# A two-layer graph attention kernel: softmax probabilities and the first layer's output split in halves before a transpose by DMA, fp16 weight halves in layer two, and a new instruction order

## What is computed

```
q, k, v = x@Wq+bq, x@Wk+bk, x@Wv+bv                     # 6 heads of 64
p0  = softmax(q k^T / 8 + where(adj, 0, -9e15))
x1  = layernorm(x + (p0 v)@Wf + bf)
h   = x1 @ W1 ;  th = tanh(h)                           # 12 heads of 32
z   = leaky(src(th) + dst(th)^T, 0.2), -999 off the mask
f   = elu(softmax(z) h + b)
g   = sigmoid(x1 @ Hw^T + Hb)
out = layernorm(x1 + g*f + (1-g)*x1)
```

## Time and profile before

| what | value |
|---|---|
| runs | 1122.74, 1123.22, 1124.8 us; median 1123.22 |
| span of the profiled execution | 1121.2 us (no run time is listed for this execution) |
| PE busy | 1047.1 us, 93% |
| PEld busy | 950.8 us, 85% |
| DVE busy | 1025.2 us, 91% |
| POOL busy | 947.2 us, 84% |
| ACT busy | 893.5 us, 80% |
| DMA, share of 16 engines | 32.7% |
| one turn in the steady part | 32.65 us |

### The profile page before, as it was taken

One profiled execution on the slowest core, in us unless ns is written; L12 is line 12 of the kernel. 1 busy time (PEld: TensorE's weight loads), 2 busy tenths in 40 slices (PEclk: granted clock), 3 DMA queues, 4 the chain that ended last, 5 costly groups with the idle time before them and its releaser, 6 DMA issues.

```text
span 1121.2 us, 32794 instructions
## 1 busy us (share of the span) xinstructions
PE 1047.1 (93%) x10890; PEld 950.8 (85%) x10890; DVE 1025.2 (91%) x2138; ACT 893.5 (80%) x1739; POOL 947.2 (84%) x781
## 2 busy tenths in 40 slices
PE   4899999999999999999999999999999999999761
PEld 4888889889898988889898888889888888988641
DVE  5589999999999999999999999999999999999854
ACT  4568888888888888888888888888888888888753
POOL 2158889988888998888899888889988888998775
PEclk9899999999999999999999999999999999999975
DMA  6103333232333333234333323433332243332232
GB/s 200 32 21 73 98 84 89 76 86 66 82 97 83 89 79 84 70 79 97 83 89 81 82 74 74 97 83 89 83 82 77 69 97 83 93 81 72 47 67 73
DMA packets 188717, 91.33 MB, mean 81 GB/s; under 512 B 158864, under 2 KB 183696, under 8 KB 188688
## 3 DMA queue, kind: packets, MB, share of 16 engines
q1 hardware_dynamic: 188688, 90.95, 32.7%
HBM read 31.61 MB, written 12.58 MB: 39 GB/s over the span
## 4 chain that ended last, share of the span: by engine, by line
PE 73%; issue 9%; DVE 8%; POOL 4%; ACT 3%; DMA 1%; DVEq 0%; SPq 0%; POOLq 0%; ACTq 0%
PE lin L459 42%; PE zp L554 6%; PE zp L613 3%; PE zp L617 3%; PE fp L583 3%; PE tp L498 3%; PE tp L567 3%; PE tp L626 2%; DVE sd L1008 2%; PE tp L595 2%; PE fp L586 2%; PE fp L640 2%; ACT th L736 1%; ACT sd_t L765 1%; POOL z L1353 1%
## 5 line engine op out<-in xcount | busy, mean ns | idle before, releaser
L1353 POOL TENSOR_TENSOR z<-z,z_max 128x1536 f32<-128x1536 f32 x64 | 176.4, 2757 | 21.3 <-DVE z_max L1136 18.9
L818 ACT ACTIVATE z<-z,log_scale 128x1536 f32<-128x1536 f32 x64 | 101.3, 1583 | 53.7 <-POOL z L1353 53.6
L1360 POOL TENSOR_TENSOR p_lo<-z,p_hi 128x1024 f16<-128x1024 f32 x64 | 137.3, 2145 | 2.3 <-ACT p_hi L824 2.3
L1365 POOL TENSOR_TENSOR f<-f,x_kept 128x384 f32<-128x384 f32 x64 | 65.0, 1016 | 72.0 <-DVE f L1168 72.0
L1318 POOL TENSOR_TENSOR prod<-th,w_sd_rows 128x768 f32<-128x768 f32 x64 | 117.9, 1842 | 6.6 <-ACT th L736 6.4
L784 ACT ACTIVATE p<-p,p_min 128x128 f32<-128x128 f32 x384 | 118.9, 399 | 4.7 <-DVE p_min L1068 4.7
L1129 DVE SCALAR_TENSOR_TENSOR z<-zp,z 128x1536 f32<-128x1536 f32 x64 | 111.9, 1748 | 2.3 <-ACT z L793 2.3
L1136 DVE TENSOR_REDUCE z_max<-z 128x12 f32<-128x1536 f32 x64 | 111.6, 1744 | 0.1
L793 ACT ACTIVATE z<-zp 128x1536 f32<-128x1536 f32 x64 | 93.2, 1457 | 17.8 <-PE zp L617 17.8
L1331 POOL TENSOR_TENSOR v_part<-v_res,v_part 128x384 bf16<-128x384 f32 x64 | 63.0, 984 | 35.8 <-ACT v_part L755 33.8
L459 PE MATMUL lin<-xt_hi,Wq_hi 128*128 128x256 f32 x288 | 81.0, 281 | 12.7 <-DVE Wk_lo L926 12.4
(11 more groups left out here) (162 smaller groups left out, 4394.2 us busy)
## 6 DMA issues: line engine op xcount, KB each, us to landing
xt_raw<-x_t SPq DMA_DIRECT2D x32, 384.0 KB, 4.0
x_raw<-x SPq DMA_DIRECT2D x32, 384.0 KB, 3.2
x_kept<-x SPq DMA_DIRECT2D x64, 192.0 KB, 2.3
out<-out_tile SPq DMA_DIRECT2D x64, 192.0 KB, 1.9
adj<-adj SPq DMA_DIRECT2D x64, 32.0 KB, 1.9
dst_row<-sd_t SPq DMA_DIRECT2D x64, 9.0 KB
p1t_hi<-p_hi SPq DMA_TRANSPOSE x64, 3.2
p1t_lo<-p_lo SPq DMA_TRANSPOSE x64, 3.1
```

Source lines behind the costliest of these rows:

```text
L818: act.activation(z[:, g, :], z[:, g, :], ACT.Exp, bias=log_scale[:, :]).then_inc(z_exp[g].sem, 1)
L1353: pool.tensor_tensor(zs, zs, z_max[:, g, :].unsqueeze(2).to_broadcast([128, H1, N]), ALU.subtract)\
L1360: pool.tensor_tensor(p1_lo[:, g, :], z[:, g, PE_HEADS * N:], p1_hi[:, g, :], ALU.subtract).then_inc(w1_lo[g].sem, 1)
```

## The change

- Layer 0's probabilities are split before they are transposed: ACT makes the f16 high half from SBUF (768 columns), DVE the low half from SBUF (768 columns, `weights0_low`), and one DMA a graph transposes both halves (`turn_weights0`, 12 blocks). The PE transposes and the copies from PSUM go.
- x1 is scaled by 1024 and split in fp16, high half on ACT (`first_high`), low half on POOL (`first_low`), and one DMA a graph transposes both (`turn_x1`, 6 blocks). W1 and Hw become fp16 halves with a scale found from their maxima.
- Layer 1 splits all 12 heads before the transpose: ACT and POOL work on 1536 columns instead of 1024, the two DMAs a graph on 12 blocks instead of 8. The PE transposes of four heads and their copies go.
- The maximum is applied in two ways: POOL adds the negative maximum for 4 heads (512 columns), and for 8 heads ACT takes one exponential each with a bias per head. DVE makes that offset (`z_offsets`, 12 columns).
- The two layer norms are applied on DVE (`norm0`, `norm1`: one tensor_scalar with mean and deviation as pointers) instead of ACT; the shifts go. Epsilon and the power -1/2 are done for both graphs in one instruction each.
- The biases of gate and projection enter as one bf16 matmul of 384 columns ahead of the product; the rows are split in three bf16 parts at the start (`row_parts`, seven instructions each for `bf` and `Hb`, after one that prepares the row; `Hb` also one small one).
- The second adjacency load and its mask go; SP copies the mask and x1 from SBUF to SBUF instead (`keep_mask`, `copy_mask`, `hold_x1`, `keep_x1`).
- Five PSUM banks serve all products and transposes (`GEN_USERS`, `BANKS`) in place of three separate sets, and every engine's list is written anew; `turn.later` is two turns back.

The core of the diff (the lists of steps are left out; three places of them follow as orders):

```diff
-PE_HEADS, DMA_HEADS = 4, 8
+SUB_HEADS = 4
...
+GEN_USERS = ("ctx0", "qk2", "ct0", "qk1", "ctx1", "pr0", "ct1", "qk0", "pr1", "sdt", "f0", "v0", "v1", "f1", "g1", "h0", "g0", "h1")
+BANKS = {"h1": 1, "g0": 4, "qk0": 3, "f1": 2, "ctx0": 3, "ct0": 2, "ctx1": 2, "ct1": 2, "pr1": 2, "qk1": 3, "v1": 3, "h0": 2}
...
+                def turn_weights0(g):
+                    sp.wait_ge(p0_low[g].sem, now(p0_low[g]))
+                    turn.apart()
+                    sp.wait_ge(ctx_mm[g].sem, prev(ctx_mm[g]))
+                    turn.apart()
+                    sp.dma_start_transpose(p0t[:, g, :, :].rearrange("p i (a n) -> p (i a) n", a=H0),
+                                           p0_part[:, g, :, :].rearrange("p i n -> p (i n)"))\
+                        .then_inc(p0_turned[g].sem, 16)
...
+                def turn_x1(g):
...
+                    sp.dma_start_transpose(x1t[:, g, :, :, :].rearrange("p i c n -> p (i c) n"),
+                                           x1_part[:, g, :, :].rearrange("p i n -> p (i n)"))\
...
-                    sp.dma_start_transpose(p1t_hi[:, g, PE_HEADS * N:].rearrange("p (a n) -> p a n", a=DMA_HEADS),
+                    sp.dma_start_transpose(p1t_hi[:, g, :].rearrange("p (a n) -> p a n", a=H1),
...
+                def hold_x1(g):
+                    sp.wait_ge(x1_ready[g].sem, prev(x1_ready[g]))
+                    turn.apart()
+                    sp.wait_ge(x1_copied[g].sem, prev(x1_copied[g]))
+                    turn.apart()
+                    sp.dma_start(x1_held[:, g, :], x1[:, g, :]).then_inc(x1_moved[g].sem, 16)
...
+            def rows_product(out, hi, lo, name, bias=None):
+                if bias:
+                    pe.matmul(out[:, 0:D], ones_bf[:, :], bias_parts[bias][:, :], start=True, stop=False)
+                return product(out[:, 0:D], hi, lo, lambda k: w_hi[name][:, k, :], lambda k: w_lo[name][:, k, :], not bias)
...
+                def weights0_high(g):
+                    act.wait_ge(sc_exp[g].sem, now(sc_exp[g]))
+                    act.wait_ge(p0_turned[g].sem, prev(p0_turned[g]))
+                    act.activation(p0_part[:, g, 0, :], p0[:, g, :], ACT.Copy, scale=PSCALE).then_inc(p0_high[g].sem, 1)
...
-                def norm0(g):
...
-                    act.activation(x1[:, g, :], y[:, g, :], ACT.Identity, bias=shift0[:, g, :], scale=rstd[:, g, :])\
-                        .then_inc(x1_ready[g].sem, 1)
...
                 def z_exponent(g):
+                    act.wait_ge(z_offset[g].sem, now(z_offset[g]))
+                    for h in range(SUB_HEADS, H1):
+                        last = act.activation(z[:, g, N * h:N * (h + 1)], z[:, g, N * h:N * (h + 1)], ACT.Exp,
+                                              bias=z_off[:, g, h:h + 1])
+                    last.then_inc(z_exp1[g].sem, 1)
+
+                def z_exponent_rest(g):
                     act.wait_ge(z_sub[g].sem, now(z_sub[g]))
-                    act.activation(z[:, g, :], z[:, g, :], ACT.Exp, bias=log_scale[:, :]).then_inc(z_exp[g].sem, 1)
+                    act.activation(z[:, g, 0:SUB_HEADS * N], z[:, g, 0:SUB_HEADS * N], ACT.Exp).then_inc(z_exp[g].sem, 1)
 
...
-                    act.activation(p1_hi[:, g, :], z[:, g, PE_HEADS * N:], ACT.Copy).then_inc(w1_hi[g].sem, 1)
-
...
-                def weights0_low(g, half):
...
-                    dve.scalar_tensor_tensor(out=p0t_lo[:, g, c], in0=bank[:, 0:3 * N], scalar=PSCALE,
-                                             in1=p0t_hi[:, g, c], op0=ALU.mult, op1=ALU.subtract)\
...
+                def weights0_low(g):
+                    dve.wait_ge(p0_high[g].sem, now(p0_high[g]))
+                    dve.wait_ge(p0_turned[g].sem, prev(p0_turned[g]))
+                    dve.scalar_tensor_tensor(out=p0_part[:, g, 1, :], in0=p0[:, g, :], scalar=PSCALE,
+                                             in1=p0_part[:, g, 0, :], op0=ALU.mult, op1=ALU.subtract)\
+                        .then_inc(p0_low[g].sem, 1)
...
-                def shift_norm0(g):
...
-                    dve.tensor_scalar(shift0[:, g, :], moments[:, g, 0:1], rstd[:, g, :], -1.0, ALU.mult, ALU.mult)\
-                        .then_inc(norm0_shift[g].sem, 1)
...
+                def variance0():
+                    for g in range(2):
+                        dve.wait_ge(y_mom[g].sem, now(y_mom[g]))
+                    for g in range(2):
+                        dve.wait_ge(x1_ready[g].sem, prev(x1_ready[g]))
+                    dve.tensor_scalar(rstd[:, :, :], moments[:, :, 1:2], EPS, X1_SCALE ** -2, ALU.add, ALU.mult)\
+                        .then_inc(y_var.sem, 2)
+
+                def norm0(g):
+                    dve.wait_ge(y_rstd.sem, now(y_rstd))
+
+                    dve.wait_ge(x1_low[g].sem, now(x1_low[g]))
+                    dve.wait_ge(x1_moved[g].sem, now(x1_moved[g]))
+                    dve.tensor_scalar(x1[:, g, :], y[:, g, :], moments[:, g, 0:1], rstd[:, g, :], ALU.subtract, ALU.mult)\
+                        .then_inc(x1_ready[g].sem, 1)
...
+                def z_offsets(g):
...
+                    dve.tensor_scalar(z_off[:, g, :], z_max[:, g, :], -1.0, math.log(PSCALE), ALU.mult, ALU.add)\
+                        .then_inc(z_offset[g].sem, 1)
...
+                def norm1(g):
+                    dve.wait_ge(y2_rstd.sem, now(y2_rstd))
+
+                    dve.wait_ge(stored[g].sem, prev(stored[g]))
+                    dve.tensor_scalar(out_tile[:, g, :], y2[:, g, :], moments2[:, g, 0:1], rstd2[:, g, :], ALU.subtract,
+                                      ALU.mult).then_inc(out_ready[g].sem, 1)
...
+                def row_parts(name, done):
+                    row = bias_row[name]
+                    parts = bias_parts[name][:, :]
...
+                    dve.tensor_copy(first, row).then_inc(rows_split.sem, 1)
+                    dve.wait_ge(rows_split.sem, done + 1)
+                    dve.tensor_tensor(rest, row, first, ALU.subtract).then_inc(rows_split.sem, 1)
...
+                    dve.scalar_tensor_tensor(out=parts, in0=second, scalar=ident[:, 1:2], in1=parts, op0=ALU.mult,
+                                             op1=ALU.add).then_inc(rows_split.sem, 1)
+                    dve.wait_ge(rows_split.sem, done + 6)
+                    return dve.scalar_tensor_tensor(out=parts, in0=rest, scalar=ident[:, 2:3], in1=parts, op0=ALU.mult,
+                                                    op1=ALU.add)
...
+                    dve.tensor_tensor(bias_row["bf"], zp[:, 2, 0:D], bias_row["bf"], ALU.add).then_inc(rows_split.sem, 1)
+                    dve.wait_ge(rows_split.sem, 1)
+                    dve.wait_ge(consts_ready.sem, 3)
+                    row_parts("bf", 1).then_inc(bf_ready.sem, 1)
...
+                def first_low(g):
+                    pool.wait_ge(x1_high[g].sem, now(x1_high[g]))
+                    pool.wait_ge(x1_turned[g].sem, prev(x1_turned[g]))
+                    pool.tensor_tensor(x1_part[:, g, 1, :], x1[:, g, :], x1_part[:, g, 0, :], ALU.subtract)\
+                        .then_inc(x1_low[g].sem, 1)
...
-                    zs = z[:, g, :].rearrange("p (a n) -> p a n", a=H1)
-                    pool.tensor_tensor(zs, zs, z_max[:, g, :].unsqueeze(2).to_broadcast([128, H1, N]), ALU.subtract)\
+                    pool.wait_ge(z_offset[g].sem, now(z_offset[g]))
+                    zs = z[:, g, 0:SUB_HEADS * N].rearrange("p (a n) -> p a n", a=SUB_HEADS)
+                    pool.tensor_tensor(zs, zs, z_off[:, g, 0:SUB_HEADS].unsqueeze(2).to_broadcast([128, SUB_HEADS, N]), ALU.add)\
...
-                    pool.tensor_tensor(p1_lo[:, g, :], z[:, g, PE_HEADS * N:], p1_hi[:, g, :], ALU.subtract).then_inc(w1_lo[g].sem, 1)
+                    pool.tensor_tensor(p1_lo[:, g, :], z[:, g, :], p1_hi[:, g, :], ALU.subtract).then_inc(w1_lo[g].sem, 1)
```

805 lines of the change are left out of this document (388 added, 417 removed).

## The result

| | before | after |
|---|---|---|
| median of four runs beside each other, us | 1123.7 (1122.74 to 1124.8) | 1279.23 (1277.08 to 1281.53) |
| span of the profiled execution, us | 1121.2 | 1275.3 |
| first `sd_t` copy on ACT, us | 67.46 | 90.17 |
| last `sd_t` copy, us | 1080.43 | 1230.39 |
| one turn, (last - first) / 31, us | 32.68 | 36.78 |

The change is slower by 13.9%, ratio 1.1389 [1.137, 1.1409]; forecast were 1184 us and a range to 1230. As a marker that both kernels have under one name I take ACT's copy of the transposed sums. The span grew by 22.7 at the start, 31 x 4.10 = 127.1 in the turns and 4.1 at the end, 153.9 of the 154.1 measured.

The account below looks back on a forecast made before the run. PE and DVE were taken as nearly full before; after the change, DVE with its waits at POOL sets the turn. 1121.2 + 31 x (34.1 - 32.62) + 15 start + 2.0 median over span = 1184 us, range 1070 to 1230.

Parts of the forecast that it names:

- the sum: Whole-kernel forecast total; its part for 31 turns growing from 32.62 to 34.1 us was 45.9 us.
- the end: Stretch after the turns: holds the same stages, so 0, give or take 4 us.
- The bare turn (30.3): DVE's turn if it waits as little as now: 32.65 - 2.4 = 30.3 us.
- rival D: Norms miss DVE's fast form: 0.8 us a turn more; 1107 us with Rival A's turn; chance 0.11 shared with Rival C.
- The waits (4.45): DVE instructions standing until POOL's running instruction ends: 4.45 us a turn, between 0 and 8.7.
- my four places: DVE waits at POOL: sums' split 2.1, first graph's `norm0` 0.5, `norm1` 0.65, two 768-column low halves 1.2 us.
- the list: DVE instructions taken to wait for POOL: those with two SBUF inputs, and the fast form with one.
- What idle time absorbs (0.6): DVE's 1.2 us of idle time a turn takes up half its own size of the waits, 0.6.
- The start (15): Before the first pair's marker: bias rows 8, weight splits 2.7, DMA transposes 5; sum 15.7, taken as 15 us.
- Rival A: DVE's instructions fall where POOL waits: 0.5 us of waits, a turn of 30.8, 1082 us; chance 0.25.
- Rival B: Every place is hit and PE held by a shared bank behind `ctx_lo`: a turn of 36, 1243 us; chance 0.12.
- Rival C: SP's transpose queue becomes late: 0.8 us on Rival A's turn, 31.6, 1107 us; chance 0.11 shared with rival D.

Follow-up runs that it names:

- e5: The changed kernel with POOL's instructions in the loop cut to 8 columns, most of their output left out: 1100.65 us, ratio 0.9809.
- e4: The changed kernel with 32 unread matmuls keeping PE at work before the transposes of the sums: 1257.77 us, ratio 1.1209.
- e11: The changed kernel with the two bias rows filled with zeros instead of prepared and split at the start: 1274.02 us, ratio 1.1347.
- e1: The changed kernel with DVE's split of the sums in one row ahead of context low half, residual and statistics: 1325.93 us, ratio 1.1816.
- e3: The changed kernel with both layer norms back on ACT, shifts on DVE, output norm and store one turn later: 1261.15 us, ratio 1.1239.
- e2: The changed kernel with each of POOL's layer 1 low halves in four instructions of 384 columns: 1199.41 us, ratio 1.0689.
- e7: The changed kernel with e2's pieces, POOL's products in two pieces and the low half of x in three: 1187.55 us, ratio 1.0583.
- e10: The changed kernel, sums' split on ACT and POOL, epsilon on POOL, products and low half of x in pieces: 1194.46 us, ratio 1.0638.
- e12: Control: the kernel before the change with POOL's low half of 1024 columns in four instructions of 256: 1136.23 us, ratio 1.012.

## Why the prediction was wrong

The direction and the mechanism were right, and so was the turn without waits; two terms were not. The steady turn, taken apart by e5 and e4:

| per steady turn, us | forecast | measured | from |
|---|---|---|---|
| without waits | 30.3 | 30.34 | e5 |
| waits at POOL, as they lengthen the turn | 4.45 - 0.6 = 3.85 | 36.44 - 30.34 = 6.10 | e4, e5 |
| lower clock of PE | 0 | 37.22 - 36.44 = 0.78 | e4 |
| sum | 34.15 | 37.22 | |

Against before's 32.65 the change would save 2.31 us a turn; the waits take 6.10 and the clock 0.78. Over all 31 turns the span grew by 127.1 us where the sum had 45.9, which is 81.2 of the miss of 95. The start, 22.7 for 15, makes 7.7 and the end, 4.1 for 0, another 4.1; the rest is 3.9 us instead of 2.0 around the profiled span.

One more row of before, the elu in the steady part (300 to 900 us), to which the second point goes back:

```profile
L1168 DVE SCALAR_TENSOR_TENSOR f<-f_neg,f 128x384 f32<-128x384 f32 x36 | 19.8, 550 | 0.0
```

- **The bare turn (30.3).** Right, in part by luck: in e5 DVE is busy 29.4 us of it and PE 29.5 (forecast 29.1 and 29.4). The four norms take 0.475 instead of 0.356 each, so **rival D** was partly true, 4 x 0.12 = 0.5; but DVE idles only 0.9 us for the 1.2 that the step kept.
- **The waits (4.45).** From the means of after less those of e5, by instructions of a turn: the cast 2.97 - 0.19 = 2.78; two first norms 0.24; two last norms 0.81; two low halves 0.75. These are my four places, 4.58, near the 4.45, and that is partly luck: forecast were 2.1, 0.5, 0.65 and 1.2. And the sums' wait came by another row: I named `sd_res` and the third part, which have two inputs, and it was the cast between them. **The step that failed is the list**: I counted two-input instructions and the norms, and left out three that were there before and ran free, or were called tiny: the elu 2 x (1.016 - 0.545) = 0.94, the minimum 2 x (0.546 - 0.355) = 0.38, the epsilon 0.859 - 0.158 = 0.70. Together 2.02, all waits 6.60. For the minimum I had even shown the row where it waits; in the change POOL works beside one of the two minima of each turn.
- **What idle time absorbs (0.6).** As forecast: in e4 rows with 6.69 of waits make a steady turn 6.10 longer.
- **The clock.** Not in my sum at all. This is the second step that failed: I had PE at 29 of 34 and did not ask what its idle time does. Behind the 1.87 us at L575 the same matmuls take 1.46 instead of 0.81, at a granted clock of 0.50, and the mean over the stretch of 183 us is 0.91. With the idle time filled (e4) it is 1.00 and a steady turn 0.78 shorter: 0.78 x 31 = 24 us, of which 21 show in the medians.
- **The start (15).** The bias rows gave 5 us or less (e11) where I took 8, so some 17 are from elsewhere, where I had 7.7. What the step did not count is work of the second pair that the new order puts ahead of the first pair's marker (part of 101 more instructions of PE). How the 17 divide between that and the transposes stays open.
- **Rival A**, that DVE's instructions miss POOL's, did not come, and in e1's order neither. **Rival B** is what came, in its place: `attend0` waits for `ctx_lo` 21.2 us in 16 turns, 1.3 a turn, and a turn of 36 was its price. But the bank is no separate cause: in e5, with POOL's work cut, this wait is gone from PE's list. **Rival C** fell with e5; in after PE waits 9.9 us in 16 turns for a transpose of layer 0, 0.6 a turn, and that wait is gone in e5 too.

The rule of the Trainium skill ("SBUF — State Buffer", Who interferes with whom) names casts and `tensor_scalar` among the forms that can exclude GpSimd, beside those with two SBUF inputs, and the traces agree: 2.97 for the cast, 0.86 for the epsilon. (The one-column shift of e3, a `tensor_scalar` too, ran at 0.20 beside POOL.) I had cited it and counted by half of it.

Why pieces help is shown (e2, e7), and that the loss is DVE's waits at POOL (e5); that a version of this change beats the kernel before is not shown. The 30.34 of e5 left POOL's work out, and every kernel that kept it stayed at a steady turn of 34.1 or more. In e1, e3, e7 and e10 a wait taken away was followed by another.

## What to carry to other kernels

When work moves between POOL and DVE, list all DVE instructions of the turn that read SBUF, the smallest too (here the long reductions and the one-column shifts kept their durations), and lay each against POOL's longest instructions; the price is what is left of POOL's instruction, not the size of DVE's. Cut a long POOL instruction into pieces only where DVE is seen waiting for it (80 us gained here, 13 lost in e12), and expect a wait that is moved by the order alone to fall on the next instruction in the list. Then ask what the newly idle engine does to its own speed: a stop of 1.9 us on PE cost another 0.78 a turn behind it.

## What the runs showed that was not expected

- Size is no protection: a cast of 48 columns took 2.97 us for 0.19, an epsilon of two columns 0.86 for 0.16. But the shift of one column ran at 0.20 in the middle of POOL's instruction (e3), and DVE's reduction of 1536 columns kept its duration: 1.740 in the steady part after, where POOL runs beside most of it, and 1.746 in e5.
- DVE gets in between two pieces of POOL, even where the second is ready: e2's cast takes 0.784, the rest of a piece of 0.92, and ends with that piece, not with all four.
- 32 matmuls a turn whose output nobody reads make the kernel 21 us faster (e4), as PE's granted clock stays at 1.00.
